# Four graph layers in one launch: products with the adjacency as the moving operand, the layer-1 chain inside one turn, and three semaphores for the row gather

## What is computed

```python
h = relu(layernorm(x)); x = x + relu(norm_adj @ (h @ K0))                 # layer 0: degrees with self-loops
h = relu(layernorm(x)); outs = [h, g@h, g@g@h, g@g@g@h]                    # layer 1: g = D^-1 (adj + I) D^-1
x = x + concat(outs) @ W.T + b
h = relu(layernorm(x)); v = neighbours of each node, dilated               # layer 2: nodes with more than 10
agg = .25*quantile(v,.25) + .5*quantile(v,.5) + .25*quantile(v,.75)        #   neighbours drop up to two of them
x = x + (relu((h + agg) @ W1 + b1) @ W2 + b2) * mask
h = relu(layernorm(x)); x = x + adj @ (h @ K3) + b3                        # layer 3
```

## Time and profile before

| | us |
|---|---|
| median of 3 runs | 2451.85 (2438.23 to 2460.9) |
| the profiled execution, its own time | 2465.37 |
| span of that execution's trace, first to last instruction | 2463.5 |
| DVE busy, PE busy, POOL busy, ACT busy | 1664.1, 1519.5, 1345.4, 469.8 |
| granted TensorE clock, mean | 0.705 of full |

### The profile page before, as it was taken

The page is one execution under the profiler, slowest core; times in us unless marked ns, Lnnn a source line. Parts: engine busy times, 40 slices in busy tenths (PEclk is TensorE's granted clock), DMA queues, the critical chain, the costliest instruction groups (busy, mean ns, idle before and its releaser), DMA issues.

```text
span 2463.5 us, 48127 instructions
## 1 busy us (share of the span) xinstructions
PE 1519.5 (62%) x20741; PEld 1193.8 (48%) x20741; DVE 1664.1 (68%) x2491; ACT 469.8 (19%) x868; POOL 1345.4 (55%) x1190
## 2 busy tenths in 40 slices
PE   2666567575676767566765756667675767664404
PEld 2555346464554646455554545446554545544303
DVE  1544777869477686948777695777868586867444
ACT  3230221203022120302122030211213130110000
POOL 1036665656646665655566565564656556666630
PEclk9776767676686667677686867767776777766555
DMA  3232232313123231313223131231323131211110
GB/s 98 70 80 30 44 71 31 86 23 94 22 42 70 32 87 22 94 21 68 46 41 77 22 94 21 51 66 27 87 29 90 24 76 21 27 21 27 20 16 5
DMA packets 106544, 121.61 MB, mean 49 GB/s; under 512 B 71326, under 2 KB 71454, under 8 KB 106270
## 3 DMA queue, kind: packets, MB, share of 16 engines
q0 software_dynamic: 36864, 37.82, 13.4%
q1 hardware_dynamic: 69406, 79.95, 10.8%
HBM read 109.23 MB, written 8.45 MB: 48 GB/s over the span
## 4 chain that ended last, share of the span: by engine, by line
DVE 31%; DMA 24%; PE 18%; issue 12%; POOL 6%; another core or an unknown queue 5%; ACT 3%; DVEq 1%; POOLq 0%; ACTq 0%; SPq 0%
DMA slots<-h_rows,row_no 23%; PE ps_prod L596 7%; POOL slots L403 6%; DVE slots L972 4%; PE ps_misc L583 3%; DVE lists L1160 2%; DVE slots L971 2%; PE ps_misc L815 2%; PE ps_tr L575 1%; DVE slots L980 1%; PE ps_misc L768 1%; ACT h_t L439 1%; DVE slots L1052 1%; DVE xc L952 1%
## 5 line engine op out<-in xcount | busy, mean ns | idle before, releaser
L403 POOL DMA_INDIRECT slots<-h_rows,row_no x1152 | 1334.9, 1159 | 1024.3 <-DMA slots<-h_rows,row_no 535.6
L596 PE MATMUL ps_prod<-mid,adj_t 128*128 128x64 bf16 x3584 | 484.1, 212 | 39.2 <-issue 38.4
L596 PE MATMUL ps_prod<-low,adj_t 128*128 128x64 bf16 x3584 | 482.7, 211 | 39.1 <-issue 38.1
L596 PEld LDWEIGHTS ps_prod<-mid,adj_t 128*128 128x128 bf16 x3584 | 379.6, 110 | 57.2 <-issue 56.1
L596 PEld LDWEIGHTS ps_prod<-low,adj_t 128*128 128x128 bf16 x3584 | 379.4, 110 | 44.8 <-issue 44.0
L596 PE MATMUL ps_prod<-y,adj_t 128*128 128x64 bf16 x2688 | 346.9, 207 | 24.8 <-issue 24.0
L596 PEld LDWEIGHTS ps_prod<-y,adj_t 128*128 128x128 bf16 x2688 | 275.6, 107 | 34.2 <-issue 33.0
L1160 DVE MAX8 lists<-ps_key 128x8 f16<-128x1024 f32 x128 | 157.8, 1233 | 58.5 <-PE ps_key L667 30.8
L575 PE MATMUL ps_tr<-ident_f,h 128*64 128x128 f32 x256 | 59.5, 413 | 212.5 <-DVEq L1317 184.6
L439 ACT ACTIVATE adj_t<-ps_tr 128x1024 bf16<-128x1024 f16 x128 | 122.6, 1025 | 265.1 <-PE ps_tr L564 264.5
L815 PE MATMUL ps_misc<-w_l_sb,h_t 65*128 65x256 f32 x256 | 132.8, 673 | 61.5 <-ACT g_l L473 49.6
(11 more groups left out here) (211 smaller groups left out, 3630.9 us busy)
## 6 DMA issues: line engine op xcount, KB each, us to landing
adj_f<-in_adj SPq DMA_DIRECT2D x128, 512.0 KB
slots<-h_rows,row_no POOLq DMA_INDIRECT x1152
x<-in_x SPq DMA_DIRECT2D x16, 256.0 KB
h_rows<-h SPq DMA_DIRECT2D x16, 256.0 KB
out<-x SPq DMA_DIRECT2D x16, 256.0 KB
y<-in_L_gnn_W SPq DMA_DIRECT2D x1, 64.0 KB
w_sb<-in_L_gnn_W SPq DMA_DIRECT2D x2, 32.0 KB
h_rows<-zeros SPq DMA_DIRECT2D x2, 32.0 KB, 1.5
```

Of the source, the lines that this page charges most:

```text
L403: pool.indirect_dma_start(out=slots[:, slot_of(par, s), t * C:(t + 1) * C], out_offset=None, in_=table[par][:, :], in_offset=bass.Indirect ...
L596: last = nc.tensor.matmul(ps_prod[:, t * C:(t + 1) * C], block_t, part(j), start=(j == 0 and k == 0), stop=(j == T - 1 and k == 2))
```

## The change

- **Products.** The features become the stationary operand and the adjacency the moving one. For each of eight tiles `j`, top half and middle half of the value lie side by side as 128 columns (`y_mid`, `z_mid`) and the low part padded with zeros to 128 (`low`, `low_z`); both are multiplied into 512 columns of `adj_t` at a time: 32 matmuls of 512 columns, in two halves, each of which fills one `ps_tr` buffer with a transposed result. ACT copies each half to `columns_t`, and eight float32 matmuls of 64 columns turn it back (`turned_back`): with `both_ident`, which adds the two halves of 64 rows, or with the layer's weights, doubled in rows, so that in layers 0 and 3 the linear layer comes after the product.
- **Self-loops** are no longer added to the adjacency by DVE (`add_loops`, `loop_diag`): in layer 0 by 16 matmuls of 128 columns with `ident_b`, in layer 1 by one float32 matmul of 512 columns (`loop_rows`).
- **Layer 1** keeps the Horner scheme, but its own terms are added on PE (`own_weights`, two float32 matmuls of 512 columns for each step); `g_l1`, L815 and its ACT copies go. All steps, `v1`, `v2`, `v3`, are now in role `b`, in one turn.
- **Roles.** The lists, norm 2, `store_h2` and the gather's issue are in `b` in place of `p`; the MLP and layer 3's product in `c` in place of `d`, where only the final addition and the store stay. `weights` stays in `p`. The sort stands in `c`, two turns behind the lists it sorts by. Norm 0 of the next graph is done at the end of a turn.
- **Order.** On DVE the turn begins with `weights`, `select_wide`, the final addition and the sort, with the steps of layers 0 and 1 between its parts, and ends with the eight lists. `slow_pe` stands between `compact` and `wide_pairs`.
- **Gather.** Three semaphores, and a wait ahead of each transfer for the transfer three before it.

```diff
-    LANES = 2
+    LANES = 3
@@ gather
-                    if issued[0] % LANES == 0:
-                        at_least(pool, one, (issued[0] // LANES) * 16)
+                    at_least(pool, one, (issued[0] // LANES) * 16)
...
-                if turn["p"] is not None:
-                    gather(turn["p"])
+                if turn["b"] is not None:
+                    gather(turn["b"])
@@ SP, per turn
-                if p is not None:
-                    store_h2(p)
                 if d is not None:
                     store_result(d)
                 if n is not None:
                     load_x(n)
                     load_adjacency(n, range(RING, T))
+                if b is not None:
+                    store_h2(b)
@@ ACT, per turn
+                    for t in range(T):
                         adjacency_columns(b, t)
+                    halves("h0", b, columns_t[:, :])
+                casts(0, 1)
+                    deviation("norm1", b)
+                casts(1, 2)
                     from_tr("select", b, ...)
+                    halves("h1", b, h1_t[:, :])
+                casts(2, 6)
+                    half_of("v1", b, 0, columns_t[:, :])
                 casts(6, 7)
+                    half_of("v1", b, 1, columns_t[:, :])
                 casts(7, 8)
                     degree_roots(n)
+                    halves("v2", b, columns_t[:, :])
+                    halves("agg", c, columns_t[0:C, :])
                     hidden(c, 0)
...
@@ PE
+            def own_weights(name, g, part):
+                for i in range(2):
+                    tr_turn(f"{name}.{i}", g)
+                    nc.tensor.matmul(tr_bank(f"{name}.{i}", g)[:, :], w_l1_sb[:, part, :],
+                                     h1_t[:, i * HALF:(i + 1) * HALF], start=True, stop=False)
+            def turned_half(name, g, i, pair_of, low_of, begun=False, loops=False):
...
+                for j in range(T):
+                    cols = slice(j * N + i * HALF, j * N + (i + 1) * HALF)
+                    nc.tensor.matmul(dst[:, :], top_halves(pair_of)[:, j, :], adj_t[g % 3][:, cols],
+                                     start=(j == 0 and not begun), stop=False)
+                    last = nc.tensor.matmul(dst[:, :], low_of[:, j, :], adj_t[g % 3][:, cols], start=False,
+                                            stop=(j == T - 1))
+                    for t in range(T // 2 if loops and j == 0 else 0):
+                        for part in (top_halves(pair_of), low_of):
+                            nc.tensor.matmul(dst[:, t * P:(t + 1) * P], part[:, i * (T // 2) + t, :], ident_b[:, :],
+                                             start=False, stop=False)
+            def turned_back(name, columns, g, weights, start):
+                for i in range(2):
+                    pe.wait_ge(tr_free, TR[f"{columns}.{i}", g] + 1)
+                    for t in range(i * (T // 2), (i + 1) * (T // 2)):
+                        last = nc.tensor.matmul(ps_prod[:, t * C:(t + 1) * C], columns_t[:, t * P:(t + 1) * P],
+                                                weights[:, :], start=start, stop=(start or t == T - 1))
+            def loop_rows(name, g):
+                nc.tensor.matmul(ps_prod[:, :], ident_f[:, :], y, start=True, stop=False)
@@ PE, per turn (b and c)
+    place_of(b); transpose_adjacency(b); turned_half("h0") x2; turned_back("lin0", "h0", w_l0_sb); compact(b)
+    slow_pe(c); wide_pairs(b); transpose_select(b); transpose_features("h1"); lin1
+    own_weights("v1"); turned_half("v1") x2; loop_rows; turned_back("v1"); spread_wide(c)
+    own_weights("v2"); turned_half("v2") x2; loop_rows; turned_back("v2"); transpose_features("agg", c)
+    own_weights("v3"); hidden_rows(c, 0); turned_half("v3", 0); hidden_rows(c, 1); turned_half("v3", 1); loop_rows
+    row_keys(b, 0); turned_back("v3"); row_keys(b, 1); cross_drops(b); row_keys(b, 2); count_over(b); mlp_rows(c)
+    row_keys(b, 3..5); turned_half("h3", 0); row_keys(b, 6); turned_half("h3", 1); row_keys(b, 7)
+    bias rows; turned_back("lin3", "h3", w_l3_sb)
@@ DVE, per turn
+    weights(p); select_wide(b); add_layer3(d); [waits of the gather(c)]; sort_1..3(c); layer0_out(b); norm_stats(b)
+    sort_4(c); norm_apply(norm1); wide_keys(b); sort_5, sort_6(c); slow_v(c); merge_first(c); propagate(b, "lin1")
+    merge_rest(c); wide_sum(c); degrees(n); propagate(b, "v1"); narrow_weighing, narrow_sum, aggregate(c)
+    propagate(b, "v2"); widest; wide_drops(b); row lists 0, 1; layer1_out(b); wide_lists(b); list 2; flag_crowds(b)
+    add_mlp(c); norm_stats(c); list 3; norm_apply(norm3); split; norm_stats(b); list 4; norm_apply(norm2); list 5
+    norm_stats(n); list 6; norm_apply(norm0); split; list 7; row_numbers(b)
```

More of the change, by code:

```diff
@@ L325, in _ @@
             for turn in turns:
-                n, p, d = [turn[role] for role in "npd"]
+                n, b, d = [turn[role] for role in "nbd"]
                 if n is not None:
@@ new lines, in _ @@
+            for turn in turns:
+                b, c = [turn[role] for role in "bc"]
+                if b is not None:
+                    place_of(b)
+                    transpose_adjacency(b)
+                    pe.wait_ge(tr_free, TR[f"adj{T - 1}", b] + 1)
+                    for i in range(2):
+                        turned_half("h0", b, i, y_mid, low, loops=True)
+                    prod_turn("lin0", b)
+                    turned_back("lin0", "h0", b, w_l0_sb, True)
+                    pe.wait_ge(select_ready, b + 1)
+                    compact(b)
@@ L821, in _ @@
                 if b is not None:
-                    product("prod1", b,
-                            (lambda j: g_top_halves(DEPTH)[:, j, :], lambda j: top_halves(mid[:, :], j),
-                             lambda j: low[:, j * C:(j + 1) * C]))
+                    own_weights("v2", b, DEPTH - 2)
+                    for i in range(2):
+                        turned_half("v2", b, i, y_mid, low, begun=True)
+                    loop_rows("v2", b)
+                    turned_back("v2", "v2", b, both_ident, False)
```

549 lines of the change are left out of this document (249 added, 300 removed).

## The result

The change made the kernel slower: 2694.52 us median (2677.0 to 2713.89) against 2456.38 (2438.23 to 2468.09), ratio 1.098, interval 1.086 to 1.110. Forecast was 2235, 9% faster. The profiled execution has a span of 2675.2 us.

A forecast was written before the change was run, and what follows sets the result against it. A turn was taken as DVE's work plus its waits for PE. 146 to first lists, first gather's turn to 250, fourteen turns of 128.5, last gather and tail gave span 2247, forecast 2235 us; range 2070 to 2370.

The forecast's parts named there:

- The gather: POOL's 72 transfers a graph: 107 us with three lanes, before 131.8; POOL's waits for its own transfers fall under 150 us.
- DVE's own work: DVE passes with hand-overs in a turn: 111.4 - 2.9 = 108.5 us; busy time falls by some 45 us in all.
- First lists: Start of the run: first lists handed over at 146 us (130 to 155), in the second turn; before 146.5, in the third.
- from the last gather's start to the end: End of the run: last gather 107 us, landing 4 later, then a tail of 87 from the last sort.
- The turn of the first gather: Turn after the first lists, without a sort, bound by the first gather: about 104 us, before 124.7.
- The waits of a turn: DVE's waits for PE's chains in each turn: 8.3 us at full clock, 57 at half, 20 taken.
- Do transfers overlap freely?: Gather step: four issues 1.24 us apart showed no queue building, so 72 x 1.46 = 105 us; otherwise 131.8.
- The clock: Sign on PE: clock above 0.75 from `v1` to lists; waits over 30 us a turn on `v1` to `v3` mean the clock.
- The gather doesn't speed up: Rival on POOL's gather: turn stays at 133 us, 105 us more in all, 2340 us; chance 0.20 - 0.03 = 0.17.
- Layer 1 at half clock: Rival on PE's four products in a row: half clock from `v1` on, waits 48, turn 156, 2620 us; chance 0.09.
- the warm case: Rival on PE: all chains at full clock, turn 117 us, 161 less in all, 2075 us; chance 0.20.
- the second limit: POOL's gather in the kernel before: 131.8 us each, so a turn can't be under some 133 us without a quicker gather.

The follow-up runs named there:

- the later sessions: Fourth to sixth sessions, before at 2359, 2336 and 2349 us: the changed kernel, nothing edited, took 2144.87, 2139.31 and 2143.07 us.
- this kind of session: First and second sessions, where the kernel before took 2456 and 2453 us; the changed kernel took 2694.52, ratio 1.098, in the first.
- the second session: Four edited kernels beside before at 2453 us; the changed kernel with two lanes as before took 2339.10 us, ratio 0.953.
- the first small kernel: Own kernel, not the four layers: 16 phases of PE matmuls beside transfers, fills or loads; 160 matmuls took 34.7 us beside transfers.

## Why the prediction was wrong

- **The gather: right.** 107 us forecast, 107.3 measured, and 107.9 to 108.6 in the later sessions; POOL's waits for its own transfers 69.3 us, under the 150 named. The 3.7 us taken for a transfer were too long: in the trace of before the landings that POOL waited for came 3.25 us after their issue in the median (2.1 to 6.4), and 0.26 more passed to the next issue. It did no harm, since by either figure three lanes keep up.
- **DVE's own work: right.** 108.5 us a turn forecast and measured (154.5 less 46.0); in all 37.5 us less, forecast 45.
- **First lists 144.1 (146), and from the last gather's start to the end 192.4 us (107 + 4 + 87 = 198): right.** The turn of the first gather was not: 176.3 (104), for the reason that follows.
- **The waits of a turn: wrong in the comparison.** 46.0 us for 20. The failed step is "Do transfers overlap freely?": the third transfer in flight was costed on POOL alone and at nothing for the other engines, because "no queue is seen to build" at four issues at the end of one gather. In its place the runs showed that in this kind of session the other engines pay for it: before with three lanes and nothing else went from 2453 to 2950 us, PE's idle time without a cause from 229 to 813, and in the changed kernel the waits ahead of `v1`, `v2` and the first two lists came to 33.7 us a turn, against 5.1 with two lanes in the second session. With two lanes all of DVE's waits were 24.9 us a turn. What had to be asked was what PE does while transfers follow each other. The profile of before held the warning: 229 us of idle time of PE without a cause, 147.6 of them in `product`, inside gathers. I had passed it over with the words "with gaps in PE's instruction supply" at `prod1`; of that stretch's 15.9 us PE was idle for 3.8. Through what the transfers hold the engines up stays open.
- **The clock: a wrong sign in the forecast.** I had written that waits of over 30 us on `v1` to `v3` would mean the clock. L1217 and L1175 together wait 280.4 + 253.7 us, 33 a turn, and from `lin1` to the lists the clock was 0.73, not above 0.75. By both marks it would be the clock. But some 10 us of PE's busy time there are all that the clock can account for, and single matmuls 1.40 us apart are no matter of clock. The marks that I had named could not tell the two causes apart.
- **The rivals.** "The gather doesn't speed up" gave 2340; the kernel in which that was made true, two lanes, took 2339 and 2360. "Layer 1 at half clock" gave 2620, near the 2694 measured, by a mechanism that was there only in part: the clock fell to 0.73 of full, not to half, and the stalls were the rest. That its figure is the nearest is luck. The rival that came true was not among them.
- **In the other sessions the forecast held.** 0.912 of before forecast, 0.909 to 0.916 measured; period 121.5 to 122.0 us with 13.5 to 13.9 of waits, for 128.5 with 20, nearer to the warm case than I had put it. That the ratios agree so closely is partly luck: the forecast was 2235 of 2452 us, and both times were some 100 us lower there, before by its stalls, the changed kernel by shorter turns than forecast. There the bound of before was the gather, which the prediction had as the second limit "hardly behind".

## What to carry to other kernels

Sum up the idle time that a profile puts down to nothing, by what runs beside it, before adding transfers beside that work: 229 us, 147.6 of them between the matmuls of a product, was the warning. A change that draws on such a resource needs runs in more than one session, since the same two kernels stood at 1.098 and at 0.909. And try parts apart: one lane more on the kernel before was +20% or -7%, the rest of the change with two lanes -5% or nothing.

## What the runs showed of the hardware

- Idle time of PE without a cause differs by more than ten times between sessions for the same program (386 and 32 us of the changed kernel). In the first two sessions it was more with more transfers in flight (before 229 with two and 813 with three; the changed kernel 34 with almost none, 54 to 88 with two, 386 with three). ACT and the hand-overs to DVE are late in the same runs.
- POOL's issues stand 1.25 us apart with DVE idle and 1.41 beside DVE passes in the first small kernel. I read from this that a waiting DVE makes transfers denser: while DVE waited from 1467.9 to 1484.1 in the timeline shown, POOL issued every 1.25 us; over whole gathers of the changed kernel it is 1.49.
- One transfer at a time takes 2.46 to 2.71 us from issue to issue in the small kernel, with one exception of 3.49; in the kernel before, the landings that POOL waited for came 2.1 to 6.4 us after their issue. The Trainium skill (DMA: Bandwidth & Descriptors, Anatomy of one DMA) gives some 2.0 us as the fixed cost; the shortest seen here is 2.13.
- An issue began 0.26 us after the landing that it waited for with one wait ahead of it, and 0.74 with two (the kernels with an added wait at every third, fourth or sixth transfer).
